# A decoder layer on one core: the setup stage is dissolved into the recurrence and the start of attention

## The reference

```python
x = _layernorm(x + attn(x, ...))          # gated linear recurrence, 16 heads of 16
x = _layernorm(x + xattn(x, ctx, ...))    # cross-attention, 16 heads, Wq, Wk, Wv, Wo with biases
x = _layernorm(x + ffn(x, ...))           # gated feed-forward, 768 wide
# recurrence: q, k, v = x@Wq, x@Wk, x@Wv; g = sigmoid(x@Wf + bf)
state = state * gt[..., None] + vt[..., None] * kt[..., None, :]
out_t = einsum('bhij,bhj->bhi', state, qt)
# then LayerNorm(out)*gamma + beta, times silu(x@Wg), times Wout
# feed-forward weights, 4 bits in blocks of 32 along the input:
s  = maximum(max(abs(wb), axis=-1) / 7, 1e-12)
wq = clip(round(wb / s), -8, 7) * s
```

## Time and profile before

| | us |
|---|---|
| median of three timed runs | 2389.9 |
| lowest, highest | 2387.39, 2391.67 |
| the profiled execution | 2383.69 |
| its span | 2382.0 |
| setup, first load to last subtraction | 0.81 to 65.84 |
| recurrence's block begins | about 66.1 |
| TensorE's first product of the recurrence | 79.65 |
| attention's first loads issued | 889.6 |
| attention's LayerNorm begins | 895.0 |

### The profile page before, as it was taken

The page is one execution under the profiler, slowest core; times in us unless marked ns, Lnnn a source line. Parts: engine busy times, 40 slices in busy tenths (PEclk is TensorE's granted clock), DMA queues, the critical chain, the costliest instruction groups (busy, mean ns, idle before and its releaser), DMA issues. The chain is left out here.

```text
span 2382.0 us, 74655 instructions
## 1 busy us (share of the span) xinstructions
PE 2162.5 (91%) x30263; PEld 1473.7 (62%) x30263; DVE 1674.3 (70%) x3031; ACT 1136.2 (48%) x1874; POOL 282.6 (12%) x272
## 2 busy tenths in 40 slices
PE   1799888998889968999999999999799999999698
PEld 1466666665666646777777777777444444444487
DVE  5577776777767765676676766666455557989897
ACT  0344443444434425666666666666311117855365
POOL 0100000000000001111111111111000004445222
PEclk9799999999999978999999999999899999999899
DMA  2010000100001001101101010110000003549674
GB/s 88 15 29 21 24 26 21 29 21 25 25 21 29 21 27 43 42 26 36 31 26 40 26 40 26 34 32 14 1 0 0 0 0 132 209 168 424 256 261 171
DMA packets 78411, 146.54 MB, mean 62 GB/s; under 512 B 10131, under 2 KB 63638, under 8 KB 78230
## 3 DMA queue, kind: packets, MB, share of 16 engines
q1 hardware_dynamic: 78230, 143.70, 17.1%
HBM read 82.84 MB, written 60.82 MB: 60 GB/s over the span
## 5 line engine op out<-in xcount | busy, mean ns | idle before, releaser
L1278 PE MATMUL ff_bank<-ff_xq,w_uh 128*128 (+1 forms) x1536 | 457.8, 380 | 2.5 <-ACT ff_whole L1387 2.5
L1278 PE MATMUL ff_bank<-ff_xq,w_ul 128*128 (+1 forms) x768 | 291.4, 379 | 0.0
L1278 PEld LDWEIGHTS ff_bank<-ff_xq,w_uh 128*128 128x128 f16 x1536 | 149.9, 98 | 181.0 <-issue 4.0
L587 ACT ACTIVATE x<-rec_e 128x512 f32<-128x512 f32 x192 | 111.3, 596 | 225.2 <-PE rec_e L476 225.2
L1592 DVE TENSOR_REDUCE ff_top<-ff_bank 128x512 f32 (+1 forms) x192 | 132.8, 692 | 116.3 <-PE ff_bank L1278 115.5
L651 DVE TENSOR_TENSOR x<-rec_x,rec_until 128x512 f32<-128x512 f32 x256 | 158.5, 680 | 23.0 <-PE rec_x L460 23.0
L1387 ACT ACTIVATE ff_whole<-ff_bank,ff_coef 128x512 int16<-128x512 f32 x192 | 124.4, 683 | 103.9 <-PE ff_bank L1278 44.2
L687 DVE TENSOR_TENSOR rec_tmp<-rec_x,x 32x256 f32<-32x256 f32 (+1 forms) x192 | 80.8, 421 | 131.0 <-PE rec_x L502 66.2
L488 PE MATMUL rec_x<-x 32*32 32x64 f32 x8192 | 147.2, 221 | 25.8 <-issue 23.0
L1063 DVE TENSOR_REDUCE mneg<-att_s 128x4 f32<-128x512 f32 x256 | 158.9, 683 | 5.4 <-PE att_s L879 4.5
L488 PEld LDWEIGHTS rec_x<-x 32*32 32x32 f32 x8192 | 127.6, 108 | 55.2 <-issue 54.9
(11 more groups left out here) (234 smaller groups left out, 4376.0 us busy)
## 6 DMA issues: line engine op xcount, KB each, us to landing
gate_scratch<-ff_out SPq DMA_DIRECT2D x28, 768.0 KB, 3.5
ff_in<-gate_scratch SPq DMA_DIRECT2D x28, 768.0 KB, 10.9
product_scratch<-ff_out SPq DMA_DIRECT2D x28, 768.0 KB, 9.7
ff_out<-product_scratch SPq DMA_DIRECT2D x28, 768.0 KB, 6.1
att_x<-in_x SPq DMA_DIRECT2D x32, 256.0 KB, 2.7
att_ctx<-in_ctx SPq DMA_DIRECT2D x32, 256.0 KB, 2.9
att_o<-rec_scratch SPq DMA_DIRECT2D x32, 256.0 KB, 3.7
out<-s_out SPq DMA_DIRECT2D x16, 512.0 KB, 3.4
```

Source lines behind the costliest of these rows:

```text
L1278: m = T.matmul(bank_[:], weights(wp, kc, a, c), tile[:, xp, kc], start=(i == 0), stop=(i == len(terms) - 1))
```

## The change

- `setup_block` is gone. The identity is made by GpSimd at the start of the recurrence's block, ahead of its masks.
- SP loads the first pair, then v, f, the bias row, q, k (each in one DMA), the second pair, down, up, gate, and then the twelve loads that attention wants. Cross-attention's raw weights wait inside `v_half`; the raw feed-forward weights have tensors that live through attention.
- `consts_ready` has two steps. The first comes after the small constants and the bias row; TensorE's first `value_gate` waits for it. The differences `sums` move into VectorE's step 0 between the floors and the split, and `exponents` wait for the second step. `marks` moves into `spare`.
- `weigh`, behind the split of step 0, takes maxima, reciprocals and scales.
- GpSimd rounds the weights: per tensor a multiplication by the reciprocals, two additions, a multiplication by the scales, each over the whole 3072 or 1536 columns.
- In attention TensorE turns the thirteen groups through four banks before its first step; ScalarE does the copies and casts, VectorE the subtractions, after `constants`; GpSimd clears `v_half` when cross-attention's groups have been turned.

```diff
-def setup_block(nc, t, w):
...
-def recurrence_block(nc, t, x_d, o_d):
+def recurrence_block(nc, t, w, x_d, o_d):
...
+        marks = spare[:, 0:2 * (NR + 3) * P].rearrange("p (b k n) -> p b k n", b=2, k=NR + 3)
...
                 load(0, 0)
+                for i, name in ((2, "v"), (3, "f")):
+                    sp.dma_start(t["w_rec"][:, :, i, :], w[name].rearrange("(c p) d -> p c d", p=P)).then_inc(qw["w_loaded"], 16)
+                sp.dma_start(t["bf_row"][:], w["bf"].partition_broadcast(3)).then_inc(qw["bf_loaded"], 16)
+                for i, name in ((0, "q"), (1, "k")):
+                    sp.dma_start(t["w_rec"][:, :, i, :], w[name].rearrange("(c p) d -> p c d", p=P)).then_inc(qw["w_loaded"], 16)
                 load(1, 1)
+                sp.dma_start(t["raw_down"][:], w["down"].rearrange("(c p) d -> p c d", p=P)).then_inc(qw["raw_loaded"], 16)
...
+                G.memset(t["half_pow"][:], -0.5)
+                pool.wait_ge(qw["part"], 1)
+                nc.gpsimd.partition_all_reduce(t["top_d"][:], cdp[:], P, RMAX).then_inc(qw["all"], 1)
+                pool.wait_ge(qw["weighed"], 1)
+                c = Chain(pool, qw["rounded"])
+                for flat, r, s in ((flat_u, ru, su), (flat_d, rd, sd)):
+                    c.did(G.tensor_tensor(blocks_of(flat), blocks_of(flat), spread(r, flat), ALU.mult))
+                    c.wait()
+                    c.did(G.tensor_scalar(flat, flat, 1.0, MAGIC, ALU.mult, ALU.add))
+                    c.wait()
+                    c.did(G.tensor_scalar(flat, flat, 1.0, -MAGIC, ALU.mult, ALU.add))
+                    c.wait()
+                    c.did(G.tensor_tensor(blocks_of(flat), blocks_of(flat), spread(s, flat), ALU.mult))
+                c.wait()
...
                 def exponents(p, s, k):
                     if k == 0:
-                        pe.wait_ge(q["consts_ready"], 1)
+                        pe.wait_ge(q["consts_ready"], 2)
...
+                pe.wait_ge(qw["ident_set"], 2)
                 turn(0, 0, 0)
+                pe.wait_ge(q["consts_ready"], 1)
+                pe.wait_ge(qw["w_loaded"], 16 * 4)
                 value_gate(0, 0)
...
                     if front:
                         floor(p, 0)
                         floor(p, 1)
+                    if not back:
+                        sums()
                     if back:
                         weighted(n, so, 0)
                         scores_out(n, 1)
                     if front:
                         split(p)
+                    if not back:
+                        weigh()
...
+                def weights():      # attention, TensorE
...
+                    for i, parts in enumerate(groups):
+                        if NR <= i < NR + WX:
+                            pe.wait_ge(qw["copied"], i - NR + 1)
+                        elif i >= NR + WX:
+                            pe.wait_ge(qw["split"], i - NR - WX + 1)
+                        for j, part in enumerate(parts):
+                            m = T.transpose(X[i % NR][:, j * P:(j + 1) * P], part, ident[:])
+                        m.then_inc(qw["turned"], 1)
...
+                def weights():      # attention, VectorE, after constants()
+                    for i in range(WU + WD):
...
+                        dve.wait_ge(qw["high"], i + 1)
+                        V.tensor_tensor(low, X[(WX + i) % NR][:], high, ALU.subtract).then_inc(qw["split"], 1)
+                    dve.wait_ge(qw["cleared"], 1)
...
+                pool.wait_ge(qw["turned"], WX)
+                G.memset(t["v_half"][:], 0.0).then_inc(qw["cleared"], 1)
...
-            setup_block(nc, t, w)
-            recurrence_block(nc, t, x_d, o_d)
+            recurrence_block(nc, t, w, x_d, o_d)
```

More of the change, by code:

```diff
@@ L332, in recurrence_block, with blocks_of, spread @@
         q = {n: sem("rec_" + n) for n in names}
+        names = "ident_set w_loaded bf_loaded raw_loaded rest_loaded part all chain weighed rounded".split()
+        qw = {n: sem("weights_" + n) for n in names}
+        def blocks_of(flat):
+            return flat.rearrange("p (n q) -> p n q", q=QBLOCK)
+        def spread(r, flat):
+            return r[:].unsqueeze(2).to_broadcast([P, flat.shape[1] // QBLOCK, QBLOCK])
         def steps(eng, step):
@@ L789, in attention_block @@
         NUM, DEN = BA[:, 0:KC * P], BA[:, KC * P:]
+        own = sb("own", [P, HH])
+        raw_x = t["v_half"].rearrange("p a b h d -> p (a b h d)")[:, 0:4 * KC * D].rearrange("p (i c d) -> p i c d", i=4, c=KC)
+        WX, WU, WD = 4, 2 * FC * KC // 4, KC * FC // 4
+        qw = {n: sem("w_" + n) for n in "turned copied high split consts ready cleared".split()}
         a_loaded = [sem(f"a_loaded{i}") for i in range(2)]
@@ L846, in turn4 @@
                     m.then_inc(done, 1)
+                def weights():
+                    raw_ff, raw_down = t["raw_ff"], t["raw_down"]
+                    cross = [[raw_x[:, i, oc, kc * P:(kc + 1) * P] for kc in range(KC) for oc in range(KC)] for i in range(WX)]
+                    up = [raw_ff[:, a, c_, kc * P:(kc + 1) * P] for kc in range(KC) for a in range(2) for c_ in range(FC)]
+                    down = [raw_down[:, oc, c_ * P:(c_ + 1) * P] for c_ in range(FC) for oc in range(KC)]
+                    groups = cross + [up[4 * g:4 * g + 4] for g in range(WU)] + [down[4 * g:4 * g + 4] for g in range(WD)]
+                    for i, parts in enumerate(groups):
[6 more added lines that the diff above has]
+                        m.then_inc(qw["turned"], 1)
+                    pe.wait_ge(qw["copied"], WX)
+                    pe.wait_ge(qw["split"], WU + WD)
+                    pe.wait_ge(qw["ready"], 1)
                 def across(bank_, wt, rhs, done):
@@ L980, in step @@
                         att_out(n0)
+                weights()
                 steps(pe, step)
@@ L1122, in apply_o @@
                     apply(os_[:, s], mv_o, rs_o, q["rstd_o"], on, q["on_ready"], p)
+                constants()
+                weights()
                 stats_o(0, 0, 0)
```

288 lines of the change are left out of this document (111 added, 177 removed).

## The result

| | before | after |
|---|---|---|
| median of four runs, us | 2388.7 | 2332.6 |
| range, us | 2387.4 to 2391.7 | 2326.2 to 2338.2 |
| profiled execution, us | 2383.7 | 2326.2 |

A forecast was written before the change was run, and what follows sets the result against it. TensorE was taken as busy over nine tenths of the span, leaving gains where it idles, chiefly the serial prologue. Terms summed to -51.4 us, from 2389.9 to 2338.5 us; range 2322 to 2357.

The forecast's parts named there:

- prologue gone: Start: without the serial setup, TensorE's first product moves from 79.65 to 10.4 us, -69.2 us.
- clock of the first products: Start: TensorE's first eight products may still run at full clock, gaining 0 to 2.6 us, taken as -1.3.
- differences moved: First pair: the differences now stand between floors and split on VectorE, delaying the split's end, +2.2 us.
- scales ahead of pair 1: Before pair 1's masks: 8.2 us of scales on VectorE delay the masking of the first scores, +0.4 us.
- rounding on GpSimd: Early recurrence: 31.6 us of GpSimd rounding makes VectorE's two-input operations wait; +10 us, bounds 0 and 31.6.
- attention's first gap: Attention's start: constants, thirteen groups of transposes and subtractions delay LayerNorm's chain; +6.5 us, bounds +4 and +9.
- the walk: Pair 1 followed step by step: VectorE's waits for GpSimd's rounding instructions add 10.7 to 12 us on the path.
- No contention: Rival, early recurrence: GpSimd's rounding does not touch VectorE's path; sum -61.4, 2328.5 us, chance 0.18.
- contention in full: Rival, early recurrence: VectorE loses 22 to 31 us on the path to GpSimd's rounding; 2351 to 2360 us, chance 0.17.
- the exposed turns: Rival, attention's start: the weight transposes are not in a gap and cost 12 us; 2344 us, chance 0.13.
- Slower than before: Rival, recurrence: VectorE's waits drop TensorE's clock to 0.50, up to 18 us more per pair; 2429 at five, chance 0.02.

The follow-up runs named there:

- no_round: The changed kernel without GpSimd's eight rounding instructions, so the feed-forward's weights stay unrounded; ratio 0.9772 to the kernel before.
- bias_first: The changed kernel with the bias row's load first in SP's queue; TensorE's first product at 10.30 us, no whole time given.
- warm: The changed kernel with TensorE transposing the identity before the first product, results unread; first four products 1.99 us, no whole time given.
- write_only: The changed kernel with GpSimd filling constants over the feed-forward's weights instead of rounding; pair 1's first sum at 52.97 us, no whole time given.
- again_beside: The changed kernel unaltered, rerun on the chip of a kernel combining several further edits; median of six 2339.3 us, ratio 0.9782 to the kernel before.
- again: The changed kernel run once more, unaltered; median 2334.3 us, ratio 0.9797 to the kernel before.

## Why the prediction was right, point by point

| term | forecast | measured |
|---|---|---|
| prologue gone | -69.2 | -69.2 |
| clock of the first products | -1.3 | +0.3 |
| differences moved | +2.2 | +2.2 |
| scales ahead of pair 1 | +0.4 | +1.0 |
| rounding on GpSimd | +10 | +9.1 by the two profiles (5.7 in pair 1, 3.4 in pair 2), +8.9 to +11.7 by no_round, one execution |
| attention's first gap | +6.5 | +1.0 in the first profile, +3.4 to +5.3 usually |

By the two profiles the change gave 57.5 us, 6.1 more than forecast. Attention's gap gives 5.5 of that, the rounding 0.9 and what no step of mine has 1.9; the clock and the scales take 2.2 back.

- **Prologue.** Whole and by the mechanism forecast. That the first product came within 0.1 us of the 10.4 was luck in part. The bias row was there at 6.75 and not 7.2, and the chain on it took 3.6 us and not 3.15; the two errors cancel. The weights I had at 7.0 to 9.6, and bias_first has the product waiting for them until 10.30. They were the second gate at almost the same time, so the error did not show.
- **Clock.** This step failed. I read the record of 1.00 at 48 to 56 us as a state in which the first products could run fast. They took 3.78. The record could not show it; what could were the durations under it, the 3.87 us of setup's first sixteen transposes among them. The Trainium skill, "TensorE: Matmul & The Clock Gate", What's actually happening, which I had set aside, was right that the throttled level is the default; warm agrees with it.
- **Differences, scales.** As worked out. A gap of 0.77 us between the last scale and the first mask was not in the sum.
- **Rounding.** The mechanism and the size held, with an error inside: GpSimd's price of 2.47 ns an element was too high. 1.05, 2.78 and 5.36 us for 512, 1536 and 3072 columns are 0.2 us + 1.68 ns an element, so a row of 512 columns overstates a long instruction; besides, that row took 1.267 us and not 1.05. It has two whole inputs where the rounding has a broadcast one; whether that is the reason is not shown. The whole began at 33.1 instead of 31 and takes 28.5 us with its waits instead of 31.6 without. The waits came where the walk had them: the second multiplication fell ahead of the second weighting (6.38 us), the first of its two alternatives, and the last short one met the total as well. Not in the walk was TensorE's clock, which fell behind the holes in pair 1. The rule of "SBUF — State Buffer", Who interferes with whom, in the Trainium skill agrees for two-input operations: none waits beside a GpSimd that only writes. It also lists casts among the operations that can take the shared pair, and the 2.79 us of write_only agree.
- **Attention.** The chain's start was forecast at 6.3 to 7.9 later; counted from the third load's issue it came 5.4 later, and 4.5 to 5.7 in the other nine executions. What the higher clock gives back I had at part of 1.6; in the first profile it was 4.4 by the first query. In the nine others the clock had fallen again, and at the query between 1.2 less and 0.7 more was lost than at the chain's start. The term was too large, and +1.0 in the profile that the table compares is luck.
- **The leftover.** By the two profiles the terms come to -69.2 + 0.3 + 2.2 + 1.0 + 9.1 + 1.0 = -55.6, and the spans differ by 57.5. The recurrence's later pairs took 0.6 more (from the first product to the last store it is 819.4 us instead of 806.1, 13.2 longer where I had 12 to 13), attention from its first query on 0.7 less. The feed-forward, 671.3 in the one profile of before and 669.0 to 669.6 in the thirteen others, gave 1.8 that no step of mine has. What that is I leave open: its instructions are the same.
- **The rivals.** No contention fell with no_round, contention in full with the 8.8, the exposed turns in part: they do cost 3.4 to 5.3 usually, not 12. Slower than before: its mechanism was there. VectorE's waits opened holes on TensorE (3.43 us in pair 1, 2.05 in pair 2), and the granted clock fell behind them, in again_beside to 0.64 over 50 to 62 us. But it came back each time: over 62 to 800 us it was 0.99 in the first profile, 0.97 in again and 0.95 in again_beside. The 3.4 pairs in that rival's line are 61.4 / 18; with the forecast's 51.4 it would have decided from 2.9 pairs on.

## What to carry to other kernels

A prologue that runs on one engine while the others wait is worth nearly its whole length, and what its work costs beside a running loop is decided by operations that hold each other off: cut such background work into short instructions. Putting it where the loop's engine reads PSUM should help too, but no run here did so: what the trace shows is that the masks, which read PSUM, kept their 2.47 us beside GpSimd's instruction of 38.54. Price a term by leaving the work out, in more than one execution, and read on past the stretch where the work runs: in three of eight executions 1.4 to 2.7 us of the rounding's price fell in the pair behind. Look at the granted clock of the engine that waits, too: a hole can cost more than its length. Before moving a gate, find the second one: here two lay within 0.2 us of each other.

## What the runs showed of the hardware

- The granted clock is recorded as 1.00 from the start of a program, while TensorE's first work takes the time of the low level: 3.78 us for four 128x512 products in the changed kernel (1.99 behind activity), 3.87 us for sixteen transposes in the kernel before.
- Behind attention's transposes TensorE was nearly idle for some 2 us; the granted clock fell again before the next products in nine of ten executions.
- GpSimd's fills of SBUF held off VectorE's cast from fp32 to f16 (2.79 instead of 0.43 us, seen once), not its two-input fp32 operations (2.28, 0.69, 1.22 and 1.76 us as without GpSimd).
- The same 30 pairs of the recurrence took 729 to 763 us in fourteen executions, 729 to 739 in one set and 748 to 763 in another, each on its own chip; the feed-forward's 669 us repeated within 0.6 in thirteen.
